# Attention block on one core: value product in one PSUM bank as three matmuls per tile, scores in two pairs of banks, exponentials of 128x1024

## The reference, cut to what matters

```python
x = ft.reshape(B, N, C)                    # B = 16, N = 32*32 = 1024 tokens, C = 512, fp32
qkv = x @ w_qkv + b_qkv                    # 8 heads, 64 wide
attn = softmax(einsum('bxhd,byhd->bxyh', q, k) * SCALE, axis=2)   # 1024 x 1024 for each head
res = einsum('bxyh,byhd->bxhd', attn, v).reshape(B, N, 512)
res = res @ w_out + b_out + x
```

## Time and profile before

| | |
|---|---|
| runs | 4126.80, 4128.93, 4134.72 us (median 4128.93) |
| span of the profiled execution | 4126.3 us, so its own time is that and the little that lies around it: the fastest run is 4126.80 |
| PE busy | 3939.8 us, 95% |
| PE weight loads | 3064.1 us, 74% |
| ACT | 3076.7 us, 75% |
| DVE | 2694.0 us, 65% |
| POOL | 2135.8 us, 52% |
| mean granted PE clock | 0.997 |

### The profile page before, as it was taken

The page is one execution under the profiler, slowest core; times in us unless marked ns, Lnnn a source line. Parts: engine busy times, 40 slices in busy tenths (PEclk is TensorE's granted clock), DMA queues, the critical chain, the costliest instruction groups (busy, mean ns, idle before and its releaser), DMA issues.

```text
span 4126.3 us, 94307 instructions
## 1 busy us (share of the span) xinstructions
PE 3939.8 (95%) x29964; PEld 3064.1 (74%) x29964; DVE 2694.0 (65%) x4395; ACT 3076.7 (75%) x5269; POOL 2135.8 (52%) x1144
## 2 busy tenths in 40 slices
PE   6999999999999999999999999999999999999999
PEld 5777777777777777777777777777777777777777
DVE  5757757576575765757657576675766757667576
ACT  4967949689495895958859588595886959769597
POOL 1645626456263563636636366363663626536265
PEclk9999999999999999999999999999999999999999
DMA  3011020110202102020021201212011121120201
GB/s 97 22 53 43 18 77 23 58 37 17 78 22 66 29 19 75 22 73 22 24 70 23 72 22 29 65 24 73 22 37 58 24 71 24 37 58 22 63 22 42
DMA packets 100814, 179.08 MB, mean 43 GB/s; under 512 B 16192, under 2 KB 16192, under 8 KB 100288
## 3 DMA queue, kind: packets, MB, share of 16 engines
q1 hardware_dynamic: 100288, 172.29, 14.7%
HBM read 71.57 MB, written 33.55 MB: 25 GB/s over the span
## 4 chain that ended last, share of the span: by engine, by line
PE 74%; issue 8%; ACT 8%; DVE 4%; POOL 4%; ACTq 0%; DMA 0%; DVEq 0%; SPq 0%; POOLq 0%
PE psum L514 33%; PE psum L545 10%; PE psum L572 8%; PE psum L595 8%; PE psum L574 7%; ACT p_hi L697 4%; PE psum L598 4%; POOL p_lo L411 4%; ACT p_full L696 3%; PE psum L528 2%; DVE max_parts L804 1%; DVE q_shift L783 1%; ACT k_lo_hi L667 1%; DVE xT_lo L767 1%; DVE q_shift L817 1%
## 5 line engine op out<-in xcount | busy, mean ns | idle before, releaser
L411 POOL TENSOR_TENSOR p_lo<-p_full,p_hi 128x1024 f16<-128x1024 f32 x752 | 1610.5, 2144 | 1452.7 <-ACT p_hi L697 1452.7
L804 DVE TENSOR_REDUCE max_parts<-psum 128x1 f32<-128x512 f32 x2048 | 1341.4, 686 | 534.0 <-PE psum L545 522.6
L696 ACT ACTIVATE p_full<-psum,prob_bias 128x512 f32<-128x512 f32 x2048 | 1434.9, 701 | 123.2 <-PE psum L574 90.6
L697 ACT ACTIVATE p_hi<-psum,prob_bias 128x512 f16<-128x512 f32 x2048 | 1435.6, 701 | 0.0
L595 PEld LDWEIGHTS psum<-v_parts,p_hi 128*128 128x128 f16 x8192 | 714.8, 97 | 284.4 <-issue 133.2
L595 PE MATMUL psum<-v_parts,p_hi 128*128 128x129 f16 x8192 | 854.4, 221 | 35.3 <-POOL p_lo L411 20.3
L572 PE MATMUL psum<-q_hi_hi,k_lo_hi 128*128 128x512 f32 x2048 | 846.2, 413 | 43.6 <-ACT p_hi L697 38.9
L598 PE MATMUL psum<-v_parts,p_lo 128*128 128x65 f16 x8192 | 819.8, 192 | 0.0
L574 PE MATMUL psum<-q_shift,k_shift 128*128 128x512 f32 x2048 | 804.7, 393 | 0.0
L545 PE MATMUL psum<-k_lo_hi,q_hi_hi 128*128 128x512 f32 x2048 | 757.1, 429 | 19.7 <-DVE q_shift L817 11.9
L598 PEld LDWEIGHTS psum<-v_parts,p_lo 128*128 128x128 f16 x8192 | 723.6, 98 | 2.4
(11 more groups left out here) (61 smaller groups left out, 4308.2 us busy)
## 6 DMA issues: line engine op xcount, KB each, us to landing
x_in<-in_x SPq DMA_DIRECT2D x128, 256.0 KB, 4.0
k_shift<-k_lo_hi SPq DMA_DIRECT2D x256, 128.0 KB, 2.2
q_hi_hi<-q_hi_hi SPq DMA_DIRECT2D x256, 128.0 KB, 2.3
y_tile<-in_x SPq DMA_DIRECT2D x128, 256.0 KB, 2.7
result<-y_tile SPq DMA_DIRECT2D x128, 256.0 KB, 2.3
o_heads<-in_L_conv_w_qkv SPq DMA_DIRECT2D x12, 256.0 KB, 4.1
o_heads<-in_L_conv_w_out SPq DMA_DIRECT2D x4, 256.0 KB, 4.3
out_bias<-in_L_conv_b_out SPq DMA_DIRECT2D x1, 256.0 KB, 6.2
```

The costliest lines, as they stand in the source:

```text
L411: nc.gpsimd.tensor_tensor(p_lo[:, s % P_SLOTS, :, :], p_full[:, s % 2, :, :], p_hi[:, s % P_SLOTS, :, :], ALU.subtract).then_inc(p_lo_read ...
L696: nc.scalar.activation(p_full[:, s % 2, n, :], score_bank(tile), ACT.Exp, scale=SCALE, bias=prob_bias[:, :])
L697: nc.scalar.activation(p_hi[:, s % P_SLOTS, n, :], score_bank(tile), ACT.Exp, scale=SCALE, bias=prob_bias[:, :]).then_inc(exp_done, 1)
L804: nc.vector.reduce_max(max_parts[:, u % 2, q_tile, k_half:k_half + 1], max_bank(w), AX.X).then_inc(max_tile_done, 1)
```

## The change

The value product goes into one bank (6) instead of two: its columns are now [sum 64 | row sum], and the low values are added into the same 64 columns by a third matmul, so for each pair of tiles there are three matmuls of 65, 64 and 65 columns. The bank so freed lets the scores have four banks, two for even and two for odd steps; a step waits once, for the exponential of the step two before it, signals once, and is exponentiated by two instructions of 128x1024. ACT's copy `unit_lo`, DVE's `o_sum` and POOL's `normalise` go away: DVE multiplies straight from PSUM into `o_heads`, after waiting for its own reciprocal (`inv_ready`). The steady fills move from bank 3 to bank 7, and the value fills of odd tiles from 7 to 3.

```diff
-SCORE_BANKS = 3
+SCORE_BANKS = (0, 1, 2, 3)
+FILL_BANK_STEADY = 7
+PV_BANK = 6
-PV_W = 2 * DIM + 1
+PV_W = DIM + 1
...
-            banks[w] = 6 + w[1] % 2
+            banks[w] = (6, 3)[w[1] % 2]
...
-        pv = psum[:, 6:8, :]
+        pv = psum[:, PV_BANK, 0:Q_TILES * PV_W].rearrange("p (t e) -> p t e", e=PV_W)
-        def score_bank(tile):
-            return psum[:, tile % SCORE_BANKS, :]
+        def score_banks(s):
+            return psum[:, KEYS_PER_STEP * (s % 2):KEYS_PER_STEP * (s % 2 + 1), :]
...
-                    for n, tile in enumerate(score_tiles(s)):
-                        pe.wait_ge(exp_done, signals_led(i, KEYS_PER_STEP * STEPS, max(tile + 1 - SCORE_BANKS, 0)))
+                    pe.wait_ge(exp_done, signals_led(i, STEPS, max(s - 1, 0)))
+                    for n in range(KEYS_PER_STEP):
...
-                        nc.tensor.matmul(score_bank(tile), k_shift[:, h % 2, keys], q_shift[:, h % 2, cols],
-                                         start=False, stop=True).then_inc(scores_ready, 1)
+                        last = nc.tensor.matmul(score_banks(s)[:, n, :], k_shift[:, h % 2, keys],
+                                                q_shift[:, h % 2, cols], start=False, stop=True)
+                    last.then_inc(scores_ready, 1)
...
-                            nc.tensor.matmul(pv[:, bank, col:col + PV_W], p_hi[:, s % P_SLOTS, n, qs],
-                                             v_parts[:, kt, h, 0:PV_W], start=kt == 0 and qt % 2 == 0,
-                                             stop=False, skip_group_check=True)
-                            last = nc.tensor.matmul(pv[:, bank, col + DIM:col + PV_W], p_lo[:, s % P_SLOTS, n, qs],
-                                                    v_parts[:, kt, h, DIM:PV_W], start=False,
-                                                    stop=kt == TOKEN_TILES - 1, skip_group_check=True)
+                            nc.tensor.matmul(pv[:, qt, :], hi, v_parts[:, kt, h, DIM:DIM + PV_W],
+                                             start=kt == 0 and qt == 0, stop=False, skip_group_check=True)
+                            nc.tensor.matmul(pv[:, qt, 0:DIM], hi, v_parts[:, kt, h, 0:DIM],
+                                             start=False, stop=False, skip_group_check=True)
+                            last = nc.tensor.matmul(pv[:, qt, :], lo, v_parts[:, kt, h, DIM:DIM + PV_W],
+                                                    start=False, stop=kt == TOKEN_TILES - 1, skip_group_check=True)
...
-                    nc.scalar.activation(p_full[:, s % 2, n, :], score_bank(tile), ACT.Exp, scale=SCALE, bias=prob_bias[:, :])
-                    nc.scalar.activation(p_hi[:, s % P_SLOTS, n, :], score_bank(tile), ACT.Exp,
+                    nc.scalar.activation(p_full[:, s % 2, :, :], score_banks(s), ACT.Exp, scale=SCALE, bias=prob_bias[:, :])
+                    nc.scalar.activation(p_hi[:, s % P_SLOTS, :, :], score_banks(s), ACT.Exp,
...
-                    nc.vector.reciprocal(inv_sum[:, :].rearrange("p (b t o) -> p b t o", b=2, o=1),
-                                         pv_columns(2 * DIM, PV_W))
-                    nc.vector.tensor_tensor(o_sum[:, :, :].rearrange("p (b t) d -> p b t d", b=2),
-                                            pv_columns(DIM, 2 * DIM),
-                                            o_lo[:, :, :].rearrange("p (b t) d -> p b t d", b=2),
-                                            ALU.add).then_inc(o_free, 1)
+                    dve.wait_ge(pv_done, signals_led(i, STEPS, STEPS_PER_UNIT * (u + 1)))
+                    nc.vector.reciprocal(inv_sum[:, :].rearrange("p (t o) -> p t o", o=1),
+                                         pv[:, :, DIM:PV_W]).then_inc(inv_ready, 1)
+                    dve.wait_ge(inv_ready, signals(i, UNITS, u + 1))
+                    nc.vector.tensor_tensor(
+                        o_heads[:, half * Q_TILES:(half + 1) * Q_TILES, h * DIM:(h + 1) * DIM], pv[:, :, 0:DIM],
+                        inv_sum[:, :].rearrange("p (t o) -> p t o", o=1).broadcast_to([P, Q_TILES, DIM]),
+                        ALU.mult).then_inc(o_ready, 1)
```

More of the change, by code:

```diff
@@ L161, in fill_banks @@
         if w[0] in ("o_transpose", "project"):
-            banks[w] = (3, 4, 5)[after % 3]
+            banks[w] = (FILL_BANK_STEADY, 4, 5)[after % 3]
             after += 1
         elif w[0] == "qk" and w[1] > 0:
-            banks[w] = 3
+            banks[w] = FILL_BANK_STEADY
         elif w in BEFORE:
@@ L310, in attention_block @@
         block = ctx.enter_context(nc.Block())
-        def score_tiles(step):
-            return [KEYS_PER_STEP * step + n for n in range(KEYS_PER_STEP)]
         def key_tile(step, n):
@@ L412, in step_lo @@
                                             p_hi[:, s % P_SLOTS, :, :], ALU.subtract).then_inc(p_lo_ready[POOL], 1)
[L414 to L421, removed]
                 def y_bias(t):
@@ L458, in claim_fill @@
                     before = last_in_bank(w)
-                    if before is None and FILL_BANK[w] < SCORE_BANKS:
-                        pe.wait_ge(exp_done, signals_led(i, KEYS_PER_STEP * STEPS, 0))
+                    if before is None and FILL_BANK[w] in SCORE_BANKS:
+                        pe.wait_ge(exp_done, signals_led(i, STEPS, 0))
                     if before is not None:
                         pe.wait_ge(fill_done, signals_led(i, FILLS, FILL_AT[before] + 1))
-                    elif FILL_BANK[w] == 3:
+                    elif FILL_BANK[w] == FILL_BANK_STEADY:
                         pe.wait_ge(fill_done, signals_led(i, FILLS, 0))
-                    if before is None and FILL_BANK[w] >= 6:
-                        pe.wait_ge(o_free, signals_led(i, UNITS, 0))
+                    if before is None and FILL_BANK[w] == PV_BANK:
+                        pe.wait_ge(o_ready, signals_led(i, UNITS, 0))
                     if before is None and FILL_BANK[w] in (4, 5):
@@ L560, in step_scores @@
                         pe.wait_ge(fill_done, signals_led(i, FILLS, FILL_AT[BEFORE[-1]] + 1))
+                    if s == 1:
+                        pe.wait_ge(fill_done, signals_led(i, FILLS, FILL_AT["v", TOKEN_TILES - 1] + 1))
                     if s % STEPS_PER_UNIT == 0:
@@ L710, in _ @@
                     if 0 <= s < STEPS:
-                        exp_tile(s, 0)
-                    if 5 <= s < STEPS and s % STEPS_PER_UNIT == 1:
-                        unit_lo((s - 5) // STEPS_PER_UNIT)
-                    if s == STEPS:
-                        unit_lo(UNITS - 1)
-                    if 0 <= s < STEPS:
-                        exp_tile(s, 1)
+                        exp_step(s)
                     for part in high_parts_in_slot(s):
@@ L759, in _ @@
             dve.wait_ge(consts_ready, 4)
-            for led in (fill_done, max_tile_done, p_lo_ready[DVE], o_free, max_ready):
+            for led in (fill_done, max_tile_done, p_lo_ready[DVE], o_ready, max_ready):
                 dve.sem_inc(led)
```

50 lines of the change are left out of this document (17 added, 33 removed).

## The result

The changed kernel takes 4103.86 us (median of 4 runs, 4103.39 to 4104.85) beside 4129.45 (4126.8 to 4134.72) of the kernel before on the same chip: a ratio of 0.9934, interval 0.9921 to 0.9946, 25.6 us faster. The forecast was 4090. Its sign and range hold. A third of the forecast gain is missing, and the traces show that over half of what did come has a source that the forecast had put at nothing, the granted clock.

A forecast was written before the change was run, and what follows sets the result against it. PE, 95% busy, bounds the kernel, with waits for ACT and POOL in three places. Per batch 1.7 + 0.3 + 0.6 - 0.25 = 2.35 us, x 16 = 38 off 4126.3, plus 2.6: 4091, called 4090; bounds 4060 to 4118, range 4040 to 4150.

The forecast's parts named there:

- The exponentials: ACT, each step: two 128x1024 instructions of 1.12 us, starts 1.00 apart, ending 0.29 us earlier; 1.7 us a batch.
- the six slots: Slots 10, 18, ..., 50 of a batch: each gives back 0.29 us, then POOL's `p_lo` is late.
- DVE at the end of a unit: DVE's multiplication waits for its reciprocal: 0.12 us added per unit, lost in two slots without fills; multiplication stays 0.39.
- Places that don't move: Slots with s % 8 = 0: fills wait for DVE's `q_lo` chain, which is not shortened; gain 0.
- Start of a batch: Slot 0's fills start earlier, once PE's wait before step 1's second score tile goes: 0.3 us, bounds 0 and 0.36.
- End of a batch: Steps 61 to 63, exponentials back to back on ACT: 0.7 us gained, bounds 0.3 and 1.1; 0.6 after a unit start.
- The value product: PE, three matmuls a pair, starts 29 ns apart: 0.70 us a step, unchanged; 0.25 us a batch allowed as loss.
- The granted clock: Half-clock stretches at 8 of 15 batch boundaries, 1.7 us lost each: change worth -13 to +12 us, 0 taken.
- Loads that pace the product: Rival, value product on PE: loads 43 ns apart, 1.03 us a step, about 4350; mild case 4160; chance 0.16.
- All waits go: Rival: all 272 us of PE's waits for ACT and POOL vanish, 3854, or 3990 with half; chance 0.10.
- The gain cancelled: Rival: six slots give nothing, through exponentials needing both tiles or a slow DVE multiplication; 4119, up to 4131; chance 0.12.
- The signs named: Marks expected in the changed profile, such as exponentials of 1.12 us, starts 29 ns apart, batches of about 253 us.

The follow-up runs named there:

- both moves and the unit's end ahead: Changed kernel, row-maximum tiles 5 and 7 a slot earlier, `p_lo` of s % 8 = 1 on POOL, unit's end before early maxima on DVE: 4077.24 us, 0.9867.
- the first experiment: Kernel before with only the value product changed to three matmuls of 65, 64 and 65 columns, in two banks: 4136.01 us, ratio 1.0006.

## Why the prediction was right, and where not

- **The exponentials.** Duration and spacing are right (1117 ns, 1.00 us). The step that failed is the one after it: that POOL's `p_lo` is late next and each of the six slots gives back 0.29. It took `q_lo` as the end of DVE's chain. But DVE's shift stands behind `q_lo`, and the second row-maximum tile needs the bank that the shift reads. Both were in reach in the trace before: the shift ended there at 1972.61 + 0.68 = 1973.29, and the second maximum (of the pair from 1973.10) followed at 1973.41.

```profile
1972.61 0.68 DVE L817 TENSOR_TENSOR q_shift<-psum,minus_block 4x512 fp32r<-4x512 f32 x1
```

Measured: 0 in place of 1.7 a batch. With DVE's chain cleared (both moves and the unit's end ahead) POOL is indeed the last to arrive, and a pair of slots such as 18 and 19 takes 5.09 us instead of 5.24: 0.15, where 0.29 was forecast. The large instructions still earn 1.83 a batch, mainly at the start, in slot 12 and in the fill-less end, of which the forecast had only the last.
- **DVE at the end of a unit.** Right in kind and nearly in size: the wait for the multiplication in slots 53 and 57 went from 0.63 to 0.78 us, 0.15 each (0.12 forecast, though the sum subtracts it once and not twice). DVE's dependent step is a gap of 0.04 us, and the multiplication took 0.42 (0.39). What was missed is that its place on DVE matters more than its length: put ahead of the maxima it is worth 20 us, about half of it at the fill-less unit ends and half in the slots of the first point.
- **Places that don't move.** Right: a slot of the kind of the earlier trace rows, 24, takes 3.98 us in both.
- **Start of a batch**. 0 instead of 0.3: the fills of the first slot come earlier, but the next slot's transpose of the maxima waits 1.43 us for DVE where PE had waited 1.06 and 0.32.
- **End of a batch**. From product 57 to 62 it is 14.30 us before and 13.49 after: 0.81 gained, 0.7 forecast.
- **The value product.** The mechanism was right, the size not: 0.65 a batch by the first experiment, 0.25 forecast, since starts go at 33, 29 and 28 ns and not all at 29. The Trainium skill ("TensorE: Matmul & The Clock Gate", section "Weight-path perf modes — Fast Weight Load (FWL) and DoubleRow") led to an estimate of 53 ns for such a load; the measured step has 24 loads and matmuls in 0.737 us, 30.7 ns each, so the trace disagrees now in an unbroken row too.
- **The granted clock.** Taken at 0 within -13 to +12; it gave the -13. This is over half of the gain, and it holds in all 15 boundaries, not as a matter of chance, so "0" was a term not worked out. Without it the kernel would have come out near 4117, at the upper end of the forecast's own 4060 to 4118: that the time came so close to 4090 is partly luck.
- **The rivals.** Loads that pace the product: refuted. All waits go: refuted, DVE took ACT's place. The gain cancelled: for the six slots just this happened, by DVE's chain as it said, though not by a slow multiplication; its 4119 is close to what the kernel would take without the help of the clock.
- **The signs named.** Right: the exponentials, no wait for ACT within a score step, slots with s % 8 = 0 as long as before. Wrong: the product of slots with s % 8 = 3 doesn't wait for POOL, matmul starts are not all 29 apart (a step takes 0.737 and not 0.70), and a batch takes 254.1 us and not 253.

## What to carry to other kernels

When a wait for one engine is taken away, follow the bank or tile to every instruction that the next matmul needs, to the last one of the chain, and not only to the first that looks late. When two buffers become one, whatever frees that buffer should be first in its engine's order: here this was worth 20 us beside the 25.6 of the change itself, though about half of it came from the rest of DVE's chain. Look for stretches of half clock and the idle time ahead of them before putting a gain down to the edited code.

## What was not expected of the hardware

- 2.0 to 2.4 us of idle time of PE at a batch boundary led to 3.4 us at 1.2 GHz in 8 of 15 boundaries when nearly all of it lay behind the transposes, and in none of 15 when a larger part of it lay ahead of them (in the changed kernel, and in the kernel before with a wait put in). Why only some of the unsplit boundaries had it is open.
- In the changed kernel the wait ahead of the transposes has no releaser in the profile (0.55 us of "issue"). PE's program of a batch is 512 matmuls longer; the kernel with the new product alone has the same length and shows such a wait in only 3 of 15 boundaries. What makes it was not tested.
- Matmuls with a load of 128x128 each start 33, 29 and 28 ns apart in a pattern of three, 30.7 on average with the first ones; what sets the pattern is open.
